# Second attention's output, router and dispatch in one stage, with expert rows gathered by a token list

## The chip, the core and the metric

One NeuronCore of a Trainium2 chip runs the whole network in one launch. Its engines work side by side and hand over by semaphores: PE (TensorE: matmuls and transposes; PEld is its weight load), DVE (VectorE), ACT (ScalarE), POOL (GpSimd) and SP (SyncE, which here only issues DMAs). The metric is the device time of one execution in microseconds (us), the median of several runs. The profile is one execution that the hardware profiler took.

## The reference

A tower of two blocks on 4 images of 512 tokens with 256 features, to which a class token per image is added after the first attention. Cut to the part that matters here:

```python
h = tok_attention(x)                                  # 16 heads of 16
h = concat([cls_tok, h], axis=1)                      # 4 x 513 tokens
h = h + rot_attention(layernorm(h))                   # causal, rotary; the "second attention"
# mixture of experts: 8 experts, 2 per token, hidden 512
x = layernorm(h).reshape(2052, 256)
topk_logits, topk_idx = top_k(x @ moe_router, 2)
weights = softmax(topk_logits)
out = zeros_like(x)
for each token t and its choice k, e = topk_idx[t, k]:
    gate, up = split(x[t] @ w13[e], 2)
    out[t] += weights[t, k] * ((silu(gate) * up) @ w2[e])
h = h + out
h = h + top_attention(layernorm(h))                   # causal, the 32 largest scores of a row only
h = h + second_experts(layernorm(h))                  # 8 experts, gated by a wide layer
```

## The kernel before

Tokens stand in 17 tiles: 16 of 128 tokens (`NT`) and one that holds the four class tokens. The program is a row of stages. A stage is a function that gives each engine its instruction list; engines run in their written order and wait on semaphores, and a barrier of all engines ends each stage. The stages in order: `begin`; `project` and `attend` for the first attention ("tok"); `attend_out` for it; `project` and `attend` for the second ("rot"); `attend_out` again; `route_moe`; `dispatch`; `run_gated_experts`; `gather_project`; `attend_top`; `last_experts`.

`attend_out` loads the output weights `wo` and bias `bo` at its start (L1812, L1813), and both PE and DVE wait for the two loads (`w_in`). Then for each tile n PE transposes the context (`turn`, L1823), ACT copies it (L1863), PE multiplies with `wo` (`project_tile`, L1832), DVE adds bias (L1897) and, for the second attention, the residual `h` (L1900), and normalises: bn_stats (L1909), bn_aggr (L1911), the root on ACT (L1869), reciprocal (L1915), and a tensor_scalar into `xn` (L1918), which is the tensor `ctx`. PE turns the normed tile (L1842) and ACT copies it to `xt` (L1876). For the second attention SP also issues the three loads of the expert weights here (`c.fetch`, 12 MB, tile `moe_w`).

`route_moe` loads the router, multiplies all 17 tiles with it (L2689: two channels of two weight loads each for a tile, so 68), and DVE finds the two largest logits of each token (`max` L2701, `max_index` L2704). `dispatch` turns the choices into places: DVE makes one-hot rows `chosen`, PE counts with a triangular and an all-ones matrix, DVE adds the counts up tile by tile (L1989, 17 steps that each wait for the one before), finds where each expert's tiles begin (L1998), and writes a row number for each of the 2 x 17 columns of tokens. Then POOL issues 34 indirect DMAs (L2036), each of which scatters 128 rows of 1 KB into the table `moe_xs` in DRAM, and waits for all of them.

`run_gated_experts` works through up to 40 tiles of 128 sorted rows, of which 38 hold tokens in this profile. SP loads rows i into one of two buffers (L2081) once PE has turned rows i-2 (`x_mm`), and stores the results y. PE turns the rows (L2120), multiplies with the owner expert's first matrix (L2131), and later with the second.

Rows that no token fills must be finite, so `attend` of the first attention clears two DRAM tables of 5 MB in the middle of its work (`clear`, tiles `moe_xs` and `last_xs`), on SP's DMA queue, ahead of the loads of later heads' queries and keys.

```python
if clear and s == G:
    for xs in c.xs.values():
        sp.dma_start(xs..., c.zeros[:, :, :].broadcast_to([P, TILES, D])).then_inc(c.xs_clear, 16)
```

Of the kernel before, what the change touches and what calls it, by code (L numbers as in the profile page):

```python
# [20 lines left out]
F32 = mybir.dt.float32  # L21
# [219 lines left out]
def project(c, tag, w, qkb, vb, cls, heads, rope=None, first=False):  # L241
# [9 lines left out]
    with c.stage() as st:  # L251
# [1517 lines left out]
def attend_out(c, tag, wo_dram, bo_dram, residual, cls, keep=None, fetch=()):  # L1769
# [6 lines left out]
    tiles = NT + (1 if cls else 0)  # L1776
    with c.stage() as st:
        wo = c.sbuf(st, f"{tag}_wo", [P, DC, D], F32)
        bo = c.sbuf(st, f"{tag}_bo", [P, D], F32)
        ctx_t = c.sbuf(st, f"{tag}_ctx_t", [P, 2, DC, P], F32)  # L1780
        summed = c.sbuf(st, f"{tag}_summed", [P, 2, D], F32)
# [5 lines left out]
        xn = keep if keep is not None else c.sbuf(st, f"{tag}_xn", [P, n_all, D], F32)  # L1787
# [3 lines left out]
        w_in = c.sem(st, f"{tag}_wo_in")  # L1791
# [4 lines left out]
        h_ok = c.sem(st, f"{tag}_h_ok")  # L1796
# [12 lines left out]

        @block.sync  # L1810
        def _(sp):
            sp.dma_start(wo[:, :, :], wo_dram).then_inc(w_in, 16)  # L1812
            sp.dma_start(bo[:, :], bo_dram.partition_broadcast(P)).then_inc(w_in, 16)  # L1813
            c.fetch(sp, fetch)

        @block.tensor
        def _(pe):
# [29 lines left out]
            pe.wait_ge(w_in, 32)  # L1847
# [42 lines left out]
        def _(dve):  # L1890
            def sums(n):
                r = rows(n)
                dve.wait_ge(o_mm, n + 1)
                if residual:
                    if n >= 2:
                        dve.wait_ge(h_ok, n - 1)
                    dve.tensor_tensor(summed[0:r, n % 2, :], ps_o[0:r, n % 2, 0:D], bo[0:r, :], ALU.add  # L1897
                                      ).then_inc(sum_ok, 1)
                    dve.wait_ge(sum_ok, n + 1)
                    dve.tensor_tensor(c.h[0:r, n, :], c.h[0:r, n, :], summed[0:r, n % 2, :], ALU.add  # L1900
                                      ).then_inc(h_ok, 1)
# [20 lines left out]
            dve.wait_ge(w_in, 32)  # L1922
# [9 lines left out]
def dispatch(c, tag, xn, idx):  # L1932
# [7 lines left out]
    n_all = NT + 1  # L1940
    with c.stage() as st:
        chosen = c.sbuf(st, f"{tag}_chosen", [P, 2, n_all, E], F32)
        both = c.sbuf(st, f"{tag}_both", [P, n_all, E], BF16)
        base = c.sbuf(st, f"{tag}_base", [P, n_all + 1, E], F32)
        begin = c.sbuf(st, f"{tag}_begin", [P, E + 1], F32)
        tiles = c.sbuf(st, f"{tag}_tiles", [P, E], F32)
        over = c.sbuf(st, f"{tag}_over", [P, E, n_all], F32)
        slot = c.sbuf(st, f"{tag}_slot", [P, n_all, E], F32)
        slot_in = c.sbuf(st, f"{tag}_slot_in", [P, n_all, E], F32)
        mine = c.sbuf(st, f"{tag}_mine", [P, 2, n_all, E], F32)  # L1950
        at = c.sbuf(st, f"{tag}_at", [P, 2, n_all], F32)
        has = c.sbuf(st, f"{tag}_has", [P, 2, n_all], F32)
# [3 lines left out]
        ps_total = c.psum(st, f"{tag}_ps_total", [P, S])  # L1956
        both_ok = c.sem(st, f"{tag}_both_ok")
        rank_mm = c.sem(st, f"{tag}_rank_mm")
        chain = c.sem(st, f"{tag}_d_chain")
        row_ok = c.sem(st, f"{tag}_row_ok")  # L1960
        sent = c.sem(st, f"{tag}_sent")
        block = st.enter_context(nc.Block())
        rank = ps_rank[:, 0:n_all * E].rearrange("p (n e) -> p n e", e=E)
        total = ps_total[:, 0:n_all * E].rearrange("p (n e) -> p n e", e=E)

        @block.vector
        def _(dve):
# [8 lines left out]
            for k in range(2):  # L1976
                then(dve.tensor_tensor(chosen[:, k, :, :],
                                       c.iota_e[:, :].rearrange("p (a e) -> p a e", a=1).broadcast_to([P, n_all, E]),
                                       idx[:, :, k:k + 1].broadcast_to([P, n_all, E]), ALU.is_equal))

                then(dve.tensor_tensor(chosen[:, k, :, :], chosen[:, k, :, :],
                                       c.valid[:, :].rearrange("p (n a) -> p n a", a=1).broadcast_to([P, n_all, E]),
                                       ALU.mult))
            dve.tensor_tensor(both[:, :, :], chosen[:, 0, :, :], chosen[:, 1, :, :], ALU.add).then_inc(both_ok, 1)
# [1201 lines left out]
```

## Time and profile before

| what | us |
|---|---|
| median of 3 runs | 1999.71 (1995.37 to 2009.43) |
| the profiled execution | 2001.38 |
| its span, first to last instruction | 1999.5 |
| second attention's `attend_out` starts | 678.22 |
| first expert tile's transpose on PE | 807.76 |

A row of the timeline gives the start, the duration, the engine, the line, the operation with its output and inputs, and in brackets how long the engine had been idle and what released it. Such times are from the span's start; the profiled execution's own time is 1.88 us longer than its span.

### The profile page before, as it was taken

How to read it: one execution, taken by the hardware profiler on the slowest of the kernel's cores; microseconds unless marked ns; L12 is line 12 of the kernel's file. 1: busy time of each engine (PE TensorE's matmuls, PEld its weight loads, DVE VectorE, ACT ScalarE, POOL GpSimd, SP SyncE). 2: the span in 40 equal slices, each digit the busy share in tenths (PEclk: the TensorE clock that was granted, in tenths of full speed). 3: DMA queues.
4: the chain of work that ended last, by engine and by line, in shares of the span. 5: the costliest groups of instructions: out<-in, count | busy, mean ns of one | idle time of the engine just before them, and what ended most of it. 6: DMA issues, size and time to landing. Idle time of an engine off the chain costs nothing. (4 is left out here: it accounts for less than half of the span.)

```text
span 1999.5 us, 35040 instructions
## 1 busy us (share of the span) xinstructions
PE 1456.5 (73%) x10387; PEld 860.4 (43%) x10420; DVE 1437.2 (72%) x4691; ACT 841.5 (42%) x2077; POOL 586.1 (29%) x1063
## 2 busy tenths in 40 slices
PE   7788887978888650799983477667776777766665
PEld 4222224534444440465642244454454454544554
DVE  4778885667777550111228799999999999999992
ACT  3366664215555420222222354455444544554532
POOL 3300000230000006000006244556555545555550
PEclk9799999978999875899996567777777666767768
DMA  5371220241221422111126310210021001300000
GB/s 165 104 254 52 58 68 9 73 117 47 49 59 36 162 99 84 38 42 47 42 66 189 81 28 9 77 28 10 20 64 49 10 20 27 107 1 12 1 1 13
DMA packets 81759, 120.86 MB, mean 60 GB/s; under 512 B 9112, under 2 KB 67392, under 8 KB 80836
## 3 DMA queue, kind: packets, MB, share of 16 engines
q1 hardware_dynamic: 78340, 110.60, 18.9%
q0 software_dynamic: 3264, 8.41, 1.3%
q8 instruction: 70, 1.15, 0.2%
q14 instruction: 85, 0.70, 0.1%
HBM read 74.11 MB, written 45.38 MB: 60 GB/s over the span
## 5 line engine op out<-in xcount | busy, mean ns | idle before, releaser
L1671 DVE MATCH_REPLACE8 top_left<-top_next,top_left 128x65 f32<-128x65 f32 (+15 forms) x768 | 322.0, 427 | 0.0
L1666 DVE MAX8 top_next<-top_left 128x8 f32<-128x65 f32 (+15 forms) x768 | 300.6, 431 | 0.1
L1126 POOL TENSOR_TENSOR top_e<-top_e,top_left 128x33 f32<-128x33 f32 (+3 forms) x254 | 188.9, 766 | 200.2 <-DVE top_left L1671 200.0
L1401 ACT ACTIVATE top_e<-top_ps_s,top_neg_max 128x129 f32<-128x129 f32 (+15 forms) x256 | 125.8, 492 | 191.0 <-POOL top_neg_max L1570 179.0
L735 DVE TENSOR_REDUCE tok_rowmax<-tok_ps_s 128x1 f32<-128x512 f32 x256 | 167.3, 688 | 34.5 <-PE tok_ps_s L577 31.9
L2231 DVE TENSOR_TENSOR moe_hid<-moe_act_gate,moe_ps_h 128x512 f32<-128x512 f32 x39 | 26.8, 688 | 220.1 <-ACT moe_act_gate L2192 220.1
L1244 PE MATMUL top_ps_pt<-ident,top_e 128*128 128x128 f32 x640 | 139.8, 348 | 27.6 <-POOL top_e L1126 12.8
L735 DVE TENSOR_REDUCE rot_rowmax<-rot_ps_s 128x1 f32<-128x128 f32 (+3 forms) x256 | 115.7, 488 | 48.6 <-PE rot_ps_s L580 45.6
L708 ACT ACTIVATE tok_et<-tok_ps_st 128x1024 f32<-128x1024 f32 x128 | 124.5, 1021 | 54.7 <-PE tok_ps_st L611 54.5
L2131 PE MATMUL moe_ps_h<-moe_w,moe_rows_t 128*128 x312 | 142.1, 598 | 0.4 <-issue 0.4
L1413 ACT ACTIVATE top_prob_t<-top_ps_pt 128x128 f32<-128x128 f32 (+3 forms) x256 | 104.8, 432 | 69.9 <-PE top_ps_pt L1244 69.3
L708 ACT ACTIVATE rot_et<-rot_ps_st 128x1024 f32<-128x1024 f32 (+3 forms) x128 | 88.0, 703 | 93.7 <-PE rot_ps_st L614 93.7
L1244 PEld LDWEIGHTS top_ps_pt<-ident,top_e 128*128 128x128 f32 x640 | 101.9, 181 | 55.1 <-issue 45.9
L1227 PE MATMUL top_ps_s<-top_ks,top_qs 96*32 96x1 bf16 (+7 forms) x1024 | 78.7, 325 | 55.0 <-DMA top_ks<-k_parts 42.8
L1653 DVE MAX8 top_raw<-top_ps_s 128x8 f32<-128x129 f32 (+15 forms) x256 | 100.8, 432 | 22.4 <-PE top_ps_s L1229 22.3
L577 PE MATMUL tok_ps_s<-tok_ks,tok_qs 96*128 96x512 bf16 x256 | 102.6, 412 | 18.9 <-DVE tok_rowmax L735 9.6
L1339 PE MATMUL top_ps_x<-gate_x_t,gate_wi 128*128 128x128 f32 (+1 forms) x512 | 99.8, 372 | 21.4 <-ACT top_next_va L1467 6.9
L1661 DVE MATCH_REPLACE8 top_left<-top_e 128x129 f32<-128x129 f32 (+15 forms) x256 | 107.5, 427 | 0.0
L1339 PEld LDWEIGHTS top_ps_x<-gate_x_t,gate_wi 128*128 128x128 f32 x512 | 93.5, 282 | 29.2 <-issue 25.3
L1258 PE MATMUL top_ps_pv<-top_prob_t,top_vs 128*32 128x128 f32 x1280 | 68.5, 361 | 50.3 <-ACT top_prob_t L1413 49.7
L1570 POOL TENSOR_SCALAR top_neg_max<-top_raw 128x1 f32<-128x1 f32 x256 | 53.5, 214 | 149.5 <-DVE top_raw L1653 145.9
L577 PE MATMUL rot_ps_s<-rot_ks,rot_qs 96*128 96x128 bf16 (+3 forms) x256 | 79.2, 332 | 24.7 <-DVE rot_rowmax L735 23.5
(355 smaller groups left out, 3141.3 us busy)
## 6 DMA issues: line engine op xcount, KB each, us to landing
moe_w<-in_moe_w SPq DMA_DIRECT2D x3, 4096.0 KB, 23.9
moe_xs<-zeros SPq DMA_DIRECT2D x1, 5120.0 KB, 20.7
last_xs<-zeros SPq DMA_DIRECT2D x1, 5120.0 KB, 33.8
moe_rows<-moe_xs SPq DMA_DIRECT2D x40, 128.0 KB, 2.2
moe_ys<-moe_y SPq DMA_DIRECT2D x38, 128.0 KB, 1.7
top_vs<-v_by_position SPq DMA_DIRECT2D x16, 256.0 KB
k_parts<-rot_parts SPq DMA_DIRECT2D x16, 192.4 KB, 3.3
rot_ks<-k_parts SPq DMA_DIRECT2D x16, 192.4 KB
```

Of the source, the lines that this page charges most:

```text
L577: mm = pe.matmul(ps_s[:, u % 2, 0:keys(qt)], lhs, k[0:PARTS * HD, h, k0:k0 + keys(qt)], start=True, stop=not causal)
L708: act.activation(et[:, kt % 2, 2 * pr:2 * pr + 2, q_from(kt):], ps_st[:, 2 * pr:2 * pr + 2, q_from(kt):], ACT.Exp).then_inc(exp_ok, 1)
L735: dve.tensor_reduce(rowmax[:, g % 2, u:u + 1], ps_s[:, u % 2, 0:keys(qt)], AX_X, ALU.max).then_inc(max_ok, 1)
L1126: eng.tensor_tensor(e[:, U % KEPT, 0:w], e[:, U % KEPT, 0:w], left[:, U % 4, 0:w], ALU.subtract).then_inc(prob_ok, 1)
L1244: mm = pe.transpose(ps_t[:, U % 2, ch * P:ch * P + P], e[:, U % KEPT, ch * P:ch * P + P], c.ident[:, :])
L1339: mm = pe.matmul(out[:, i * P:i * P + r], gate_wi[:, ch, f * P:f * P + P], x_t[:, ch, 0:r], start=ch == 0, stop=ch == DC - 1)
L1401: act.activation(e[:, U % KEPT, 0:keys(U)], row(U), ACT.Exp, bias=neg_max[:, U % 4:U % 4 + 1]).then_inc(e_ok, 1)
L1413: act.activation(prob_t[:, m % 2, 0:J + 1, :, QS * (U % 4):QS * (U % 4) + QS], ps_t[:, U % 2, 0:P * (J + 1)].rearrange("p (c h q) -> p c h ...
L1661: dve.match_replace(left[:, U % 4, 0:w], e8[:, U % 4, :], e[:, U % KEPT, 0:w], 0.0).then_inc(pick, 1)
L1666: dve.max(next8[:, U % 2, step // 2, :], left[:, U % 4, 0:keys(U)]).then_inc(pick, 1)
L1671: ins = dve.match_replace(left[:, U % 4, 0:w], next8[:, U % 2, step // 2 - 1, :], left[:, U % 4, 0:w], 0.0)
L2131: mm = pe.matmul(ps_h[:, k % 2, half, :], rows_t[:, k % 2, ch, :], w1[:, ch, bass.ds(e, 1), half * S:half * S + S].rearrange("p a n -> p ( ...
```

## The change

1. `attend_out`, `route_moe` and `dispatch` of the second attention become one stage, `attend_dispatch`. In one loop over tiles PE turns and projects tile n, turns the normed tile n-2, and routes tile n-3; DVE adds, normalises, and searches the two largest of tile n-4. Tiles are counted in groups (4, 4, 4, 3, 2): when a group has been searched, DVE makes its one-hot rows, POOL adds them up over tiles, PE ranks them, and DVE works out the place within an expert's tile, two iterations later.
2. There is no scatter and no table `moe_xs`. The normed rows go to DRAM in token order (`rot_normed`, 17 plain stores on SP). PE multiplies one-hot places with one-hot tiles, weighted with the token's number, which gives a list `ids`: for each expert tile and row, the token. `run_gated_experts` has POOL gather 128 rows by that list for each tile, into the same two buffers; SP keeps the stores.
3. Only `last_xs` is cleared.
4. Output weights, biases and the router are fetched with the other weights during the first attention. The second attention's bias is added to `h` by POOL during its `project` stage, so that DVE adds the projection straight to `h`.

```diff
 # project, POOL's list
+            if bias is not None:
+                pool.wait_ge(c.fetched, fetched)
...
                     pool.tensor_tensor(lo[:, k, span(k)], rest[:, k % 2, span(k)], mid[:, k, span(k)],
                                        ALU.subtract).then_inc(lo_ok, 1)
+                    if bias is not None:
+                        h = c.h[:, bass.ds(b * NQ + k, 1), :].rearrange("p a n -> p (a n)")
+                        pool.tensor_tensor(h, h, bias[:, :], ALU.add)
 # attend_out
-            sp.dma_start(wo[:, :, :], wo_dram).then_inc(w_in, 16)
-            sp.dma_start(bo[:, :], bo_dram.partition_broadcast(P)).then_inc(w_in, 16)
-            c.fetch(sp, fetch)
...
-            pe.wait_ge(w_in, 32)
+            pe.wait_ge(c.fetched, 16 * arrived)
 # attend_dispatch (new)
+    groups = [(0, 4), (4, 8), (8, 12), (12, 15), (15, n_all)]
+    chunks = [(0, 8), (8, 15), (15, n_all)]
...
+            c.fetch(sp, fetch)
+            for n in range(n_all):
+                r = rows(n)
+                sp.wait_ge(xn_ok, n + 1)
+                sp.dma_start(c.xn[n * P:n * P + r, :], c.ctx[0:r, n, :]).then_inc(x_sent, 16)
+            sp.wait_ge(x_sent, 16 * n_all)
...
+            def route(n):
+                pe.wait_ge(x_out, n + 1)
+                if n:
+                    pe.wait_ge(at_ok, n)
+                for ch in range(DC):
+                    mm = pe.matmul(ps_l[0:rows(n), 0:E], x_t[:, n % 2, ch, 0:rows(n)], router[:, ch, :],
+                                   start=ch == 0, stop=ch == DC - 1)
+                mm.then_inc(l_mm, 1)
+            def count(g):
+                a, b = groups[g]
+                if g < len(groups) - 1:
+                    pe.wait_ge(ahead_ok, b)
...
+                if g:
+                    pe.wait_ge(place_ok, g)
+                pe.matmul(ps_rank[:, 0:(b - a) * E], c.before[:, :], both[:, a:b, :], start=True, stop=False)
+                pe.matmul(ps_rank[:, 0:(b - a) * E], c.ones_bf[:, :], ahead[:, a:b, :], start=False, stop=True
+                          ).then_inc(rank_mm, 1)
...
+                            mm = pe.matmul(ps_ids[:, 0:2 * TILES], at_place[0:r, k, n, :],
+                                           by_row[0:r, k, n, :, :].rearrange("p a t -> p (a t)"),
+                                           start=n == 0 and k == 0, stop=n == n_all - 1 and k == 1)
...
+            for n in range(n_all + 4):
+                if n + 1 < n_all:
+                    turn(n + 1)
+                if n < n_all:
+                    project_tile(n)
+                if 2 <= n < n_all + 2:
+                    turn_normed(n - 2)
+                if 3 <= n < n_all + 3:
+                    route(n - 3)
+                if n - 5 in group_end and group_end[n - 5] < len(groups) - 1:
+                    count(group_end[n - 5])
+            count(len(groups) - 1)
+            row_numbers()
...
+            for n in range(n_all + 6):
+                if 4 <= n < n_all + 4:
+                    search(n - 4)
+                if n < n_all:
+                    sums(n)
+                    moments(n)
+                if 1 <= n <= n_all:
+                    normalise(n - 1)
+                if n - 4 in group_end:
+                    choose(group_end[n - 4])
+                if n - 6 in group_end and group_end[n - 6] < len(groups) - 1:
+                    places(group_end[n - 6])
+                    spread_places(group_end[n - 6])
 # dispatch, POOL's list
-                        pool.indirect_dma_start(
-                            out=c.xs[tag][:, :], out_offset=bass.IndirectOffsetOnAxis(ap=c.row[:, k, n:n + 1], axis=0),
-                            in_=xn[:, n, :], in_offset=None, bounds_check=TILES * P - 1, oob_is_err=False
-                        ).then_inc(sent, 16)
-                pool.wait_ge(sent, 16 * 2 * n_all)
 # run_gated_experts
-                sp.dma_start(rows[:, i % 2, :], c.xs[tag][i * P:(i + 1) * P, :]).then_inc(rows_in[i % 2], 16)
+            def gather_rows(i):
+                pool.indirect_dma_start(
+                    out=rows[:, i % 2, :], out_offset=None, in_=c.xn[:, :],
+                    in_offset=bass.IndirectOffsetOnAxis(ap=c.ids[:, i:i + 1], axis=0),
+                    bounds_check=NT * P + B - 1, oob_is_err=False).then_inc(rows_in[i % 2], 16)
+            gather_rows(0)
+            gather_rows(1)
+            used = used_tiles(pool)
+            for i in range(2, TILES):
+                if i < SURE_TILES + 2:
+                    pool.wait_ge(x_mm, i - 1)
+                    gather_rows(i)
 # program
-        c.xs = {t: nc.dram_tensor(f"{t}_xs", [TILES * P, D], F32, kind="Internal").ap() for t in ("moe", "last")}
+        c.xs = {t: nc.dram_tensor(f"{t}_xs", [TILES * P, D], F32, kind="Internal").ap() for t in ("last",)}
+        c.xn = nc.dram_tensor("rot_normed", [NT * P + B, D], F32, kind="Internal").ap()
+                get_rot = get_wo_tok + get_rot + get_wo_rot + [(router[:, :, :], a["router"])]
```

DVE's list in the middle of the second attention's output, before (one tile: add the bias, add to `h`, moments, and the normalising of the tile before):

```order
L1897 TENSOR_TENSOR rot_summed<-rot_ps_o,rot_bo 128x256
L1900 TENSOR_TENSOR h<-h,rot_summed 128x256
L1909 BN_STATS rot_stats<-h 128x6
L1911 BN_AGGR rot_mv<-rot_stats 128x2
L1915 RECIPROCAL rot_rstd<-rot_std 128x1
L1918 TENSOR_SCALAR ctx<-h,rot_mv,rot_rstd 128x256
```

and after, at tile 9, whose iteration also closes the second iteration after the first group's search (`rot_ps_l` holds one tile's logits):

```order
L2198 MAX rot_top<-rot_ps_l 128x8
L2200 MAX_INDEX rot_top_at<-rot_top,rot_ps_l 128x8
L2177 TENSOR_TENSOR h<-h,rot_ps_o 128x256
L2181 BN_STATS rot_stats<-h 128x6
L2183 BN_AGGR rot_mv<-rot_stats 128x2
L2187 RECIPROCAL rot_rstd<-rot_std 128x1
L2190 TENSOR_SCALAR ctx<-h,rot_mv,rot_rstd 128x256
L2227 TENSOR_TENSOR rot_mine<-rot_chosen,rot_ps_rank 128x2x32
L2231 TENSOR_REDUCE rot_rank<-rot_mine 128x2x4
L2232 TENSOR_TENSOR rot_whole<-rot_rank,steps 128x2x64
L2237 TENSOR_REDUCE rot_turn_no<-rot_whole 128x2x4
L2238 SCALAR_TENSOR_TENSOR rot_place<-rot_turn_no,rot_rank 128x2x4
```

One add went, and the search of the tile four back and, once in a group, the places came between a tile's normalising and the next tile's add.

POOL's list from the dispatch on, before (34 scatters behind the row numbers, and nothing in the expert stage):

```order
L2032 TENSOR_LOAD used
L2032 ISA x2
L2033 COMPARE_AND_BRANCH
L2036 DMA moe_xs<-ctx,row 5120x256 x34
L2033 UNCONDITIONAL_BRANCH
```

and after, from the last group that POOL adds up:

```order
L2156 TENSOR_TENSOR rot_both<-rot_chosen 128x24
L2162 TENSOR_TENSOR rot_ahead<-rot_ahead,rot_both 128x8 x3
L89 UNCONDITIONAL_BRANCH
L92 ISA
L2378 UNCONDITIONAL_BRANCH
L2381 DMA moe_rows<-rot_normed,ids 128x256 x2
L2355 TENSOR_LOAD used
L2355 ISA x2
L2381 DMA moe_rows<-rot_normed,ids 128x256 x32
```

The scatters are gone from between the stages; the expert stage's row loads came from SP to POOL, two ahead of the loop and the rest behind `x_mm`.

## Rows read from the trace of the kernel before

**Rows 1.** Timeline at the seams, from the second attention's output to the first expert tile.

```profile
678.22 0.36 SPq L1812 DMA_DIRECT2D rot_wo<-in_rot_wo  x1
...
683.51 0.69 PE L1823 MATMUL rot_ps_t<-ident,ctx 128*128 128x128 f32 x2 [4.59 <-DMA rot_bo<-in_rot_bo]
...
722.92 14.01 PE L2689 MATMUL moe_ps_l<-moe_router,xt 128*128 128x8 f32 x68 [2.63 <-DMA moe_router<-in_router]
...
742.73 0.30 DVE L1977 TENSOR_TENSOR moe_chosen<-iota_e,idx 128x136 f32<-128x136 f32 x1 [0.76 <-PEq L93]
...
805.65 4.38 SPq L2081 DMA_DIRECT2D moe_rows<-moe_xs  x4
807.76 0.29 PEld L2120 LDWEIGHTS moe_ps_x<-ident,moe_rows 128*128 128x128 f32 x2 [63.21 <-DMA moe_rows<-moe_xs]
```

**Rows 2.** Tiles moe_xs and moe_rows: ns min/median/max, first and last start in us.

```profile
L2036 POOL DMA_INDIRECT moe_xs<-ctx,row x34: 974/976/1270, 756.2 to 798.8; - x34
...
L2120 PE MATMUL moe_ps_x<-ident,moe_rows x80: 272/273/475, 807.8 to 1037.9; 128*128 128x128 f32 x80
```

**Rows 3.** Windows: PE, PEld, DVE, ACT, POOL busy, PE clock, DMA share, GB/s.

```profile
690.00:700.00 10.00, 7.57 (x41) 5.31 (x41) 9.10 (x31) 4.03 (x15) 0.00 (x0) 1.00 0.98 420
...
710.00:720.00 10.00, 6.70 (x34) 3.75 (x32) 9.24 (x31) 3.49 (x14) 0.00 (x0) 1.00 0.14 57
...
730.00:740.00 10.00, 6.92 (x36) 6.79 (x36) 3.01 (x41) 0.00 (x0) 0.00 (x0) 0.50 0.00 1
```

**Rows 4.** Timeline of SP, then of POOL, in the first attention.

```profile
98.19 14.80 SPq L547 DMA_DIRECT2D last_xs<-zeros  x1
...
137.14 0.62 POOL L562 COPY tok_vs<-tok_va 128x512 f32<-128x512 f32 x1 [13.66 <-PE tok_ps_pv L625]
155.73 0.62 POOL L562 COPY tok_vs<-tok_va 128x512 f32<-128x512 f32 x1 [17.97 <-PE tok_ps_pv L625]
```

**Rows 5.** Timeline: start of the first attention's output; end of the second's projection.

```profile
317.54 0.69 PE L1823 MATMUL tok_ps_t<-ident,ctx 128*128 128x128 f32 x2 [2.94 <-DMA tok_bo<-in_tok_bo]
...
426.26 2.18 POOL L451 TENSOR_TENSOR rot_parts<-rot_rest,rot_parts 128x513 bf16<-128x513 f32 x2 [3.16 <-ACT rot_parts L424]
```

**Rows 6.** Timeline of the second attention's output: first projection, and one later tile.

```profile
683.99 1.91 PE L1832 MATMUL rot_ps_o<-rot_wo,rot_ctx_t 128*128 128x256 f32 x4
...
711.50 0.42 DVE L1897 TENSOR_TENSOR rot_summed<-rot_ps_o,rot_bo 128x256 f32<-128x256 f32 x1
...
711.64 0.44 PE L1842 MATMUL rot_ps_x<-ident,ctx 128*128 128x128 f32 x2 [0.44 <-DVE ctx L1918]
...
711.95 0.43 DVE L1900 TENSOR_TENSOR h<-h,rot_summed 128x256 f32<-128x256 f32 x1
...
712.13 1.03 PE L1832 MATMUL rot_ps_o<-rot_wo,rot_ctx_t 128*128 128x256 f32 x4
...
713.47 0.42 DVE L1897 TENSOR_TENSOR rot_summed<-rot_ps_o,rot_bo 128x256 f32<-128x256 f32 x1
```

**Rows 7.** Timeline of DVE: a wide copy, the largest of 17 tiles, the chained sums.

```profile
435.02 1.23 DVE L824 COPY rot_v_cls<-rot_ps_st 128x1024 f32<-128x1024 f32 x1 [3.43 <-PE rot_ps_st L674]
...
737.35 1.25 DVE L2701 MAX8 moe_top<-moe_logits 128x8 f32<-128x8 f32 x17
...
744.94 3.30 DVE L1989 TENSOR_TENSOR moe_base<-moe_base,moe_ps_total 128x8 f32<-128x8 f32 x17 [0.56 <-PE moe_ps_total L2025]
```

**Rows 8.** Groups of POOL by form: busy us, mean ns of one, idle before.

```profile
L1141 POOL TENSOR_TENSOR h<-h,top_summed 128x256 f32<-128x256 f32 x15 | 11.2, 749 | 1.2
...
L1126 POOL TENSOR_TENSOR top_e<-top_e,top_left 128x33 f32<-128x33 f32 x16 | 4.1, 259 | 9.8 <-DVE top_left L1671 9.8
```

**Rows 9.** Timeline of POOL: indirect gathers in the stage behind the experts.

```profile
1046.61 1.36 POOL L2820 DMA_INDIRECT moe_got<-moe_ys,row  x1 [0.93 <-POOL moe_got L2814]
...
1051.40 1.00 POOL L2820 DMA_INDIRECT moe_got<-moe_ys,row  x1 [0.30 <-issue]
```

**Rows 10.** Tile moe_got: the 34 gathers from issue to landing.

```profile
DMA to landing us min/median/max: 2.7/3.1/7.7
```

More of the change, by code:

```diff
@@ L238, in load_step, with project @@
     load_keys(sp, c, b, g, k, loaded)
-def project(c, tag, w, qkb, vb, cls, heads, rope=None, first=False):
+def project(c, tag, w, qkb, vb, cls, heads, rope=None, first=False, bias=None):
     nc = c.nc
@@ L1974, in then @@
                 dve.wait_ge(chain, done[0])
[L1976 to L1983, printed above, removed]
@@ L1995, in _ @@
-            then(dve.tensor_reduce(tiles[:, :], over[:, :, :], AX_X, ALU.add))
-            then(dve.memset(begin[:, 0:1], 0.0))
-            for e in range(E):
-                then(dve.tensor_tensor(begin[:, e + 1:e + 2], begin[:, e:e + 1], tiles[:, e:e + 1], ALU.add))
-            then(dve.scalar_tensor_tensor(
-                out=slot_in[:, :, :], in0=begin[:, 0:E].rearrange("p (a e) -> p a e", a=1).broadcast_to([P, n_all, E]),
-                scalar=float(P), in1=base[:, 0:n_all, :], op0=ALU.mult, op1=ALU.add))
@@ L2002, in _ @@
-            then(dve.tensor_tensor(slot[:, :, :], slot_in[:, :, :], rank, ALU.add))
-            for k in range(2):
-                then(dve.tensor_tensor(mine[:, k, :, :], chosen[:, k, :, :], slot[:, :, :], ALU.mult))
-            then(dve.tensor_reduce(at[:, :, :], mine[:, :, :, :], AX_X, ALU.add))
-            then(dve.tensor_reduce(has[:, :, :], chosen[:, :, :, :], AX_X, ALU.add))
-            then(dve.scalar_tensor_tensor(out=at[:, :, :], in0=has[:, :, :], scalar=-float(NOWHERE),
-                                          in1=at[:, :, :], op0=ALU.mult, op1=ALU.add))
@@ new lines, in _ @@
+            then(dve.tensor_reduce(begin[:, :], shares[:, :, :], AX_X, ALU.add))
+            places(len(groups) - 1)
+            spread_places(len(groups) - 1)
+            then(dve.tensor_tensor(
+                mine[:, :, :, :], chosen[:, :, :, :], begin[:, 0:E].rearrange("p (k n e) -> p k n e", k=1, n=1
+                                                                              ).broadcast_to([P, 2, n_all, E]), ALU.mult))
+            then(dve.tensor_reduce(first_tile[:, :, :], mine[:, :, :, :], AX_X, ALU.add))
@@ new lines, in _ @@
+            then(dve.tensor_copy(c.used[:, :], begin[:, E:E + 1]))
+            then(dve.scalar_tensor_tensor(out=row_f[:, :, :], in0=tile_no[:, :, :], scalar=float(P), in1=place[:, :, :],
+                                          op0=ALU.mult, op1=ALU.add))
+            then(dve.tensor_tensor(c.row[:, :, :], row_f[:, :, :], nowhere[:, :].rearrange(
+                "p (k n) -> p k n", k=1).broadcast_to([P, 2, n_all]), ALU.add))
+            dve.wait_ge(ratio_ok, 1)
+            then(dve.tensor_scalar(one_more[:, :], ratio[:, :], 1.0, None, ALU.add))
@@ L2043, in run_gated_experts @@
+            then(dve.reciprocal(weight[:, 0, :], one_more[:, :]))
+            then(dve.tensor_tensor(weight[:, 1, :], ratio[:, :], weight[:, 0, :], ALU.mult))
+            dve.wait_ge(ids_mm, 1)
+            then(dve.tensor_copy(row_low[:, :], ps_ids[:, 0:TILES]))
+            then(dve.scalar_tensor_tensor(out=c.ids[:, :], in0=ps_ids[:, TILES:2 * TILES], scalar=float(P),
+                                          in1=row_low[:, :], op0=ALU.mult, op1=ALU.add))
 def run_gated_experts(c, tag, w1, w2, hidden):
@@ L3087, in program @@
             fetch = [(w13[:, ch], a["moe_w13"][:, ch]) for ch in range(DC)] + [(w2[:, :, :, :], a["moe_w2"])]
[L3088 to L3090 removed]
+            attend_dispatch(c, "rot", *wo_rot, router, idx, weight, fetch)
             run_gated_experts(c, "moe", w13, w2, MOE_HIDDEN)
```

475 lines of the change are left out of this document (315 added, 160 removed).

## Prediction

> **What bounds the kernel now.** I read the chain of waits first, and it is no help here: its pieces lie in the last part of the span, in the attention with 32 scores per row, which the change doesn't touch. So the places touched are read one by one from the timeline, by what each waits for last. In the seams of the middle [rows 1] the second attention's output stage begins at 678.22, PE then stands 4.59 us for the bias, the router multiplies from 722.92, dispatch starts at 742.73, the next stage's loads leave at 805.65 and PE turns the first expert rows at 807.76. These 129.5 us (807.76 - 678.22) are a serial piece: no other stage runs beside it. The windows [rows 3] show who fills it: DVE has 9.1 of 10 us while tiles are normalised, PE 6.9 of 10 while it routes at the lower clock, and nobody but POOL works in the scatter, 34 issues from 756.2 to 798.8 [rows 2]. Behind it the expert tiles run at (1037.9 - 807.8) / 39 = 5.9 us each [rows 2], on PE.
>
> **The change, part by part.** The sum is made against the profiled execution, 2001.4; the median is 1.7 lower.
>
> *A, one cleared table less.* The second clear kept SP's queue for 14.80 us, and the loads of later heads stood behind it. POOL's copies, one per head group, come every 13.66 + 0.62 = 14.3 us, but once 17.97 + 0.62 = 18.6 [rows 4]. With half the bytes the queue should be free before the keys are wanted: -4.3. If another thing made that step long, 0. I take -4.3.
>
> *B, weights of the first output stage.* PE stood 2.94 us for the bias [rows 5]. It now arrives in the first attention, on a queue idle by then: -2.9.
>
> *C, the bias on POOL.* 16 adds of 128x256 at 0.75 [rows 8], each behind a subtraction of 1.1 (two in 2.18 [rows 5]), plus one for the class rows. All but the last lie beside PE's projections. At the end the last subtraction starts one add later, 0.75, and an add and the class add follow, 1.5, beside SP's last stores: between 0 and +1.5, I take +0.6. What is queued behind is the barrier.
>
> *D, the fused stage.* Its length from start to the first expert transpose is built up.
>
> Start: turn, copy and first projection at the lower clock. Before, PE's second turn took 0.69 and the projection 1.91 [rows 6]; with 0.7 for the first turn and its copy, the first add is 3.3 us after the start.
>
> A tile: DVE needs 713.47 - 711.50 = 1.97 [rows 6], less one add (711.95 - 711.50 = 0.45), plus the search. A chained small operation takes 3.30 / 17 = 0.19 [rows 7], so two cost some 0.35: 1.87. PE needs from 711.64 to 712.13 + 1.03, so 1.52 [rows 6], plus four router weight loads: 14.01 / 68 = 0.21 each at the lower clock [rows 1, 3], half of that at the upper, 0.41. That is 1.93 on PE. PE waits for DVE's search (one buffer of logits) and DVE for PE's projection, but turn and projection lie between, so the two overlap; with 0.2 for handing over I take 2.15. Seventeen: 36.6.
>
> Groups: eight DVE instructions with 8 to 1024 columns. A cost of 0.19 plus 1.05 ns per column fits both ends ([rows 7]: 1.23 for 1024). 8 x 0.19 + 1488 x 1.05 ns = 3.1; three of these inside the loop, 9.3.
>
> POOL's counting: one add of 32 columns at 0.26 [rows 8] and four smaller ones in chain, 1.3 us, for which PE's `count` waits, with the next turn and projection queued behind it. PE would have been busy some 0.5 of that: +0.9 for each of three groups, 2.7.
>
> End: four more iterations without a projection, 0.9 each, 3.6. Then 43 DVE instructions in one chain (last group, first tiles, one-hot tiles, list): 43 x 0.19 + 6370 columns x 1.05 ns = 14.9. The 34 matmuls that make the list take at most 0.21 each; 16 of them run while DVE builds the second chunk, and the rest beside what DVE still has to do. Only 0.6 sticks out. Barrier 0.8 (the idle time at 742.73 [rows 1]), POOL's start 0.6, and the first gather, 3.1 from issue to landing [rows 10], with ends 2.7 and 7.7. The Trainium skill (DMA: Bandwidth & Descriptors, Anatomy of one DMA) fits such a DMA by 2.0 us plus its bytes at 436 GB/s, 2.3 us for 128 KB as an estimate; by it the sum would be 0.8 lower, and the rows say no.
>
> Sum: 3.3 + 36.6 + 9.3 + 2.7 + 3.6 + 14.9 + 0.6 + 0.8 + 0.6 + 3.1 = 75.5, so D is 129.5 - 75.5 = -54.0.
>
> What hides what: the expert weights are loaded at the start as before, at 420 GB/s, and the rate is down to 57 by the window after 710 [rows 3], more than 30 us before the stage's new end at 678.2 - 4.3 - 2.9 + 0.6 + 75.5 = 747. The 17 stores of normed rows queue behind them on SP and have the whole tail to land. In the expert loop a gather is issued when rows i-2 are turned, and its rows are needed two tiles later, 11.8 us; it takes 1.0 to issue and 2.7 to 7.7 to land [rows 9, 10]: nothing. SP's loads before landed in that shadow too. Behind the experts nothing is changed.
>
> Total: -4.3 - 2.9 + 0.6 - 54.0 = -60.6; 2001.4 - 60.6 = 1940.8, on the medians 1939.
>
> Bounds: A and C, +5.2 at worst. The tile on DVE's 1.87 alone gives -4.8, and if the groups' work fits in the time DVE waits for PE, -4.8 more; POOL's counting hidden, -2.7. The list's matmuls all behind DVE, +3; a first gather of 7.7, +4.6.
>
> **The rivals.**
>
> *1. The engines take turns.* Five engines in fixed order with two buffers each, and one for the logits: if DVE's search waits for PE's route, and PE's next projection waits for DVE, a tile costs PE's route plus DVE's work plus a handover, some 0.41 + 1.87 + 0.8 = 3.1 instead of 2.15: 17 x 0.95 = +16, 1955. For it: in the stage before, PE waits 0.44 us for DVE's normalised tile in every tile [rows 6]. Against: the turn and the projection don't depend on the search. Chance 0.20.
>
> *2. PE stays at the lower clock.* Then projection, two transposes and router cost 0.88 + 0.6 + 0.41 more per tile [rows 6], 17 x 1.9 = +32: 1971. Against: PE had 1.00 with 7.57 of 10 us busy [rows 3], and gets more work per tile. For it: the same PE with 6.92 busy of narrow router matmuls stood at 0.50 [rows 3]. Chance 0.06.
>
> *3. Slower than before: the gathers bind the experts.* Two buffers and one POOL instruction per tile: with a gather of G us from release to landing, a tile can't be shorter than (G + 0.4) / 2. Up to G = 11.4 it is hidden. To eat 60.6 us over 38 tiles it takes 1.6 us more a tile, G = 14.6; at 16, the tile is 8.2 and the time 1939 + 38 x 2.3 = 2026. For it: POOL makes the descriptors now, where SP loaded plain blocks, and a gather beside DVE's copies took 1.36 instead of 1.00 [rows 9]. Against: 7.7 was the longest of 34. The Trainium skill warns of just this (SBUF - State Buffer, Who interferes with whom, and the "DVE blocks DMA" trap): a two-port copy of DVE locks GpSimd out while it writes descriptors, and a DMA of 0.62 us took 3.1. The trace agrees in kind, with 0.36 us rather than 2.5. By the page a gather's issue, made five times longer, would be 5.0 as an estimate; this and 7.7 is 12.7, and only gathers that meet both ends would show. Chance 0.03.
>
> *4. The change doesn't do what it says*: the saving of the scatter is given back in the list's making, tail 25 us longer than added up (each chained instruction 0.77 instead of 0.19): 1964. Against: the chain of 17 has no such gap [rows 7]. Chance 0.03.
>
> **How the numbers follow.** The forecast has 0.68, the rivals 0.20, 0.06, 0.03 and 0.03. The likeliest is 1939. Its own range by the bounds, not all at once, is 1929 to 1950; with the first rival the range is 1928 to 1960. What a measurement can tell here is about 1%, 20 us. All cases but the third end below 1980; with a little kept for a stall that no row shows, faster 0.95, same 0.03, slower 0.02.
>
> **What would show it.** In the profile after: from the start of the fused stage to the first expert transpose 75 us (rival 1: over 88); DVE's adds 2.1 to 2.3 us apart outside the groups; PE's clock 1.00 in the middle of the stage (rival 2: 0.50); POOL's 40 gathers spread over the expert stage with PE's tiles still 5.9 us apart (rival 3: over 7); no copy of POOL in the first attention 18 us behind the one before; PE's first turn of the first output stage without a wait for a DMA. The prediction is wrong if the stage is over 95 us long, if the expert tiles slow down, or if anything behind 1044 takes another time than before.

## The result and the profile after

The changed kernel takes 1929.3 us (median of 4 runs, 1927.7 to 1935.0) where the kernel before took 2001.3: the ratio is 0.965, 95% interval 0.962 to 0.968. That is 72 us less; forecast were 60.6 less and 1939, with a range of 1928 to 1960. The profiled execution of after took 1935.0, the longest of the four, with a span of 1933.3. It is compared stage by stage with the one profile of before.

The timeline of after at the seams (start, duration, engine, line, operation, idle time before):

```profile
307.36 1.08 PE L1820 MATMUL tok_ps_t<-ident,ctx 128*128 128x128 f32 x4 [1.63 <-PEq L93]
...
340.14 3.30 POOL L446 MEMSET rot_va<- 128x3840 f32 x1 [89.67 <-POOLq L93]
...
423.03 1.80 POOL L563 MEMSET rot_ks<- 32x2052 bf16 x1 [1.10 <-POOLq L93]
...
667.56 0.63 PE L2030 MATMUL rot_ps_t<-ident,ctx 128*128 128x128 f32 x4 [2.44 <-PEq L93]
...
670.34 0.42 DVE L2177 TENSOR_TENSOR h<-h,rot_ps_o 128x256 f32<-128x256 f32 x1 [2.23 <-PE rot_ps_o L2039]
...
719.43 0.15 DVE L2200 FIND_INDEX8 rot_top_at<-rot_top,rot_ps_l 4x8 uint32<-4x8 f32 x1
...
733.69 0.20 DVE L2318 SCALAR_TENSOR_TENSOR ids<-rot_ps_t,rot_row_low 128x40 uint32<-128x40 f32 x1
735.86 1.30 POOL L2381 DMA_INDIRECT moe_rows<-rot_normed,ids  x1 [17.17 <-issue]
...
739.15 0.69 PE L2405 MATMUL moe_ps_x<-ident,moe_rows 128*128 128x128 f32 x2 [7.27 <-DMA moe_rows<-rot_normed,ids]
...
977.48 0.35 SPq L98 DMA_DIRECT2D top_w<-in_top_w  x1
```

The fused stage begins at 667.56 and the first expert rows are turned at 739.15: 71.6 us, where [rows 1] give 129.5. Its last search ends at 719.58, the list is written at 733.89, and POOL's first gather starts 1.97 later. All stages, each from such seams, with the letters of the prediction's terms:

| stage | before | after | difference | forecast |
|---|---|---|---|---|
| up to the first attention | 66.7 | 65.7 | -1.0 | 0 |
| first attention (A) | 247.5 | 241.7 | -5.8 | -4.3 |
| first output stage (B) | 35.1 | 32.8 | -2.3 | -2.9 |
| second projection (C) | 82.0 | 82.9 | +0.9 | +0.6 |
| second attention | 247.0 | 244.5 | -2.5 | 0 |
| output, router, dispatch (D) | 129.5 | 71.6 | -57.9 | -54.0 |
| experts, to the next stage's first load | 236.6 | 238.3 | +1.7 | 0 |
| the rest | 955.2 | 955.8 | +0.7 | 0 |
| span | 1999.5 | 1933.3 | -66.2 | -60.6 |

In the expert stage the gathers land in the shadow, as the view of the tile `moe_rows` shows (durations in ns; of the 40, all but the first took 992 to 998):

```profile
L2405 PE MATMUL moe_ps_x<-ident,moe_rows x80: 272/273/476, 739.1 to 970.6; 128*128 128x128 f32 x80
L2381 POOL DMA_INDIRECT moe_rows<-rot_normed,ids x40: 992/992/1299, 735.9 to 960.0; - x40
...
DMA to landing us min/median/max: 2.7/2.8/3.6
```

The tiles are (970.6 - 739.1) / 39 = 5.94 us apart (before 5.9, [rows 2]). The +1.7 of the expert stage isn't the gathers' doing as far as the runs show: with plain loads again (`e1_scatter`, below) the stage takes 237.3, and in the other kernels with one gather a tile, issued in that stage, 236.8 to 238.3.

### The profile page after: what moved, and what is told of

It reads as the page before. It is cut to its first block and busy times, and to the rows that moved or that the text cites. A ratio compares the mean times of both kernels' runs of the same rounds, so it can differ in the third digit from the quotient of the medians.

```text
span 1933.3 us, 35202 instructions
## 1 busy us (share of the span) xinstructions
PE 1459.6 (75%) x10462; PEld 857.0 (44%) x10463; DVE 1442.6 (75%) x4694; ACT 842.7 (44%) x2080; POOL 607.8 (31%) x1108
## 5 line engine op out<-in xcount | busy, mean ns | idle before, releaser
L1234 PE MATMUL top_ps_s<-top_ks,top_qs 96*32 96x1 bf16 (+7 forms) x1024 | 77.8, 322 | 55.2 <-DMA top_ks<-k_parts 43.5
L1346 PE MATMUL top_ps_x<-gate_x_t,gate_wi 128*128 128x128 f32 (+1 forms) x512 | 95.1, 359 | 22.8 <-ACT top_next_va L1474 8.2
L2381 POOL DMA_INDIRECT moe_rows<-rot_normed,ids x40 | 40.0, 1001 | 202.3 <-PE moe_ps_x L2405 184.8
L1346 PEld LDWEIGHTS top_ps_x<-gate_x_t,gate_wi 128*128 128x128 f32 x512 | 88.9, 270 | 30.2 <-issue 26.2
```

Of the source, the lines that this page charges most:

```text
L1346: mm = pe.matmul(out[:, i * P:i * P + r], gate_wi[:, ch, f * P:f * P + P], x_t[:, ch, 0:r], start=ch == 0, stop=ch == DC - 1)
```

## The experiments

**The theory** after the result: fusion and list each give a part of D, the list the larger; in a clean tile, one without a group's work, PE (some 1.93, as added up) and DVE (1.87, measured where it has no gap) run beside each other; the clear and the late weights were real costs; gathers have room. **The rivals**: the gain is the fusion's alone; the engines take turns; the long step of the first attention was an accident of one execution; gathers are near to binding. The edits are shown shortened.

How far a stage repeats has to be known first. `e10_unchanged` is the changed kernel once more.

> The changed kernel as it is, beside the run before it on the same chip: 1930. Its second profile shows how far each stage's length repeats: the stage 71.5 within 1.5, the second attention anywhere from 240 to 246.

It took 1928.5 (1924.8 to 1936.6), ratio 0.963 (0.961 to 0.965), and its fused stage 68.8 instead of 71.6, further off than the 1.5 that were expected. In six profiles whose loop is that of the changed kernel, the loop (from the first turn to the start of the last search) took 48.5 to 51.6 us, mean 50.3; the tail (from there to the first expert rows) took 20.0 to 20.2 where that too is unchanged. The difference goes with PE's clock behind a group's chain. A granted clock of 1.00 is TensorE's upper level, 2.4 GHz, and 0.50 the lower one, 1.2. The windows of after, and then of the repeat, whose stage begins 2.0 us later (columns: stretch, busy time of PE, PEld, DVE, ACT and POOL, granted clock, DMA share, GB/s):

```profile
685.00:690.00 5.00, 4.27 (x29) 3.28 (x27) 3.95 (x20) 1.90 (x8) 1.04 (x5) 1.00 1.08 465
690.00:695.00 5.00, 2.49 (x10) 2.18 (x11) 4.28 (x17) 1.24 (x5) 0.00 (x0) 0.78 0.97 416
695.00:700.00 5.00, 5.00 (x21) 4.16 (x20) 2.60 (x12) 0.85 (x3) 1.04 (x5) 0.54 0.84 271
```

```profile
680.00:685.00 5.00, 4.99 (x32) 3.81 (x31) 4.40 (x21) 2.22 (x9) 0.00 (x0) 1.00 0.98 421
685.00:690.00 5.00, 4.25 (x29) 3.44 (x29) 3.98 (x21) 2.08 (x8) 1.04 (x5) 1.00 1.01 433
690.00:695.00 5.00, 2.49 (x19) 1.84 (x18) 4.59 (x16) 0.84 (x3) 0.00 (x0) 1.00 0.98 416
695.00:700.00 5.00, 4.25 (x30) 3.38 (x30) 4.57 (x22) 1.92 (x8) 1.04 (x5) 1.00 1.12 419
```

In the repeat's first window, where no group is worked on, PE is busy for 4.99 of 5 us. In both executions PE stands for 2.51 us in the window from 690, until the search that is queued behind the first group's chain is done. In after the clock then falls, and DVE's next two adds come 3.49 and 3.31 us apart; in the repeat it stays, and they come 1.99 and 2.22 apart. A stage length is trusted below only beyond this spread.

**The scatter put back** (`e1_scatter`): the fused stage without the list; what follows is as before.

```diff
-            row_numbers()                      # PE: one-hot products
-            spread_places(g), at_tile, by_row  # DVE and ACT: their factors
+            for n, k: pool.indirect_dma_start(out=c.xs["moe"], ... c.row[:, k, n:n + 1], in_=c.ctx[:, n, :])
```

> The changed kernel with the list of tokens undone: the fused stage scatters its normalised rows into a cleared table, 34 issues by POOL, and the expert tiles load plain blocks, as before; the second table is cleared again in the first attention. Theory (fusion and list each give a part, the list the larger one): the loop 52.1 less three spreads of 1.2, 48.5; the tail 14.3 less the spreads and the list's tiles, 8.6; then the scatter as before, 51.6 from its first issue to the first expert transpose (807.8 - 756.2). Stage 109 us instead of 71.6, the first attention 5.8 longer for the clear: 1929 + 37 + 6 = 1972. Rival (the gain is the fusion's, and a scatter behind it would be cheap too, POOL's issues taking 1.0 instead of 1.25 in a quiet stage): stage under 98, time under 1960.

Measured 1971.8, ratio 0.987 (0.984 to 0.990). The stage took 107.0, the first attention, with both clears, 246.1. From its timeline, first and last scatter, then the loads and PE:

```profile
720.06 1.27 POOL L2147 DMA_INDIRECT moe_xs<-ctx,row  x1 [11.32 <-issue]
721.63 0.98 POOL L2147 DMA_INDIRECT moe_xs<-ctx,row  x1 [0.30 <-issue]
...
762.51 0.97 POOL L2147 DMA_INDIRECT moe_xs<-ctx,row  x1 [0.31 <-issue]
769.36 4.33 SPq L2332 DMA_DIRECT2D moe_rows<-moe_xs  x4
771.42 0.29 PEld L2371 LDWEIGHTS moe_ps_x<-ident,moe_rows 128*128 128x128 f32 x2 [59.00 <-DMA moe_rows<-moe_xs]
```

The scatter's 51.4 us (771.42 - 720.06) are those of before. So fusing gives 129.5 - 107.0 = 22.5 us, and the list another 107.0 - 71.6 = 35.4 (38.2 against the repeat), plus the clear. The rival (under 98) falls.

**The clear and the late weights put back** (`e2_clear_and_weights`):

```diff
-        c.xs = {... for t in ("last",)}
+        c.xs = {... for t in ("moe", "last")}
-                get_rot = get_wo_tok + get_rot + ...
+                attend_out(c, "tok", *wo_tok, get_wo_tok)    # SP fetches them there
```

> The changed kernel with terms A and B undone, everything else left: two tables are cleared in the first attention, and the weights of the first output stage are fetched in that stage. Theory: POOL's copy that came 18.6 us behind the one before and the later one of 15.6 both return, the first attention takes 247.5 instead of 241.7 (+5.8); the first output stage takes 35.1 instead of 32.8 (+2.3); time 1937. Rival (the long step was an accident of that one execution): attention 241.7 within 0.5, only the +2.3 shows, 1932.

Measured 1940.6 in one run; first attention 248.3, first output stage 34.8. Its timeline, SP's queue and POOL's copies:

```profile
96.14 14.36 SPq L554 DMA_DIRECT2D last_xs<-zeros  x1
110.60 14.33 SPq L223 DMA_DIRECT2D tok_qs<-q_parts  x3
...
134.14 0.61 POOL L569 COPY tok_vs<-tok_va 128x512 f32<-128x512 f32 x1 [13.65 <-PE tok_ps_pv L632]
153.43 0.62 POOL L569 COPY tok_vs<-tok_va 128x512 f32<-128x512 f32 x1 [18.68 <-PE tok_ps_pv L632]
```

the late copy of `e1_scatter`, which has both clears too, but the weights early:

```profile
155.07 0.61 POOL L569 COPY tok_vs<-tok_va 128x512 f32<-128x512 f32 x1 [18.04 <-PE tok_ps_pv L632]
```

and that of after:

```profile
107.55 5.08 SPq L223 DMA_DIRECT2D tok_qs<-q_parts  x3
...
136.04 0.61 POOL L569 COPY tok_vs<-tok_va 128x512 f32<-128x512 f32 x1 [13.66 <-PE tok_ps_pv L632]
150.30 0.61 POOL L569 COPY tok_vs<-tok_va 128x512 f32<-128x512 f32 x1 [13.65 <-PE tok_ps_pv L632]
```

With both clears a step of 19.3 us is back, and one of 18.7 in `e1_scatter`: 5.0 and 4.4 over the usual 14.3. The loads behind the clears keep the queue for 14.33 instead of 5.08. The attention takes 248.3 and 246.1, which is 2.8 to 7.3 us longer than the 241.0 to 243.3 of the kernels with one clear. The long step was no accident, and since `e1_scatter` shows it with the weights early, it belongs to the clear. The second long step of before (15.6) returned in neither run. The first output stage is 2.2 longer than one at the same clock (32.6 in `e5_search_first`, both at 0.90).

**The bias on DVE** (`e3_bias_dve`): one more add per tile there, none on POOL.

```diff
-                dve.tensor_tensor(h, h, ps_o, ALU.add)
+                dve.tensor_tensor(summed, ps_o, bo, ALU.add)
+                dve.tensor_tensor(h, h, summed, ALU.add)
```

> The changed kernel with term C undone: no bias adds on POOL in the second projection; DVE adds the bias in the fused stage, one more add of 0.45 us a tile. Theory (PE's 1.93 and DVE's 1.85 a tile run beside each other, with little slack on DVE): a clean tile 2.30 instead of 1.97, the loop 6 us longer, the projection 0.9 shorter, time +5. Rival 1 of the prediction (engines in turns, everything adds up): +7.7 in the loop. Rival (PE alone sets the pace and DVE has room): loop unchanged.

Measured 1939.0 in one run; loop 57.3, projection 81.3. Clean tiles of this kernel in the timeline, and then of after:

```profile
671.65 0.40 DVE L2182 TENSOR_TENSOR rot_summed<-rot_ps_o,rot_bo 128x256 f32<-128x256 f32 x1
...
673.96 0.40 DVE L2182 TENSOR_TENSOR rot_summed<-rot_ps_o,rot_bo 128x256 f32<-128x256 f32 x1
```

```profile
679.59 0.40 DVE L2177 TENSOR_TENSOR h<-h,rot_ps_o 128x256 f32<-128x256 f32 x1
...
681.58 0.42 DVE L2177 TENSOR_TENSOR h<-h,rot_ps_o 128x256 f32<-128x256 f32 x1
```

2.31 against 1.99 apart (four tiles in a row: 2.32 against 1.96 in the mean). 0.44 us more DVE work lengthen a tile by 0.36: DVE had some 0.1 of slack beside PE, as the theory has it; PE alone doesn't set the pace. The loop is 5.7 longer than that of after, 7.0 than the mean of 50.3: the rival's 7.7 isn't excluded by that sum, but by the tile, which would be 3.1 us and one add more if the engines took turns.

**The group's chain out of the loop** (`e4_places_last`):

```diff
-                if n - 6 in group_end and ...: places(g); spread_places(g)   # in the loop
+            for g in range(len(groups) - 1): places(g); spread_places(g)     # behind it
```

> The changed kernel with the work on ranks and places of the first four groups moved out of the loop to its end (same instructions, later). Theory (a group's DVE chain of 3.1 us inside the loop costs more than itself, because PE stands 2.5 us behind the search, and its clock falls for the next two tiles): the loop loses 3 x 4.5 = 13, the tail gains 9, the stage is 4 us shorter, PE's clock 1.00 through the loop. Rival (DVE's work is what counts, wherever it stands): stage the same within 1 us. Second rival (the clock falls in the loop in any case): stage longer by up to 4.

Measured 1935.2 in one run; loop 40.6, tail 27.6, stage 68.1. The clock stays at 1.00 until 5 us before the loop's end. The chains of three groups cost some 10 us in the loop and 7.6 behind it: the sign of the theory, but 68.1 is within 0.7 of the shortest unchanged stage, so its 4 us aren't shown.

**The search ahead of the chain** (`e5_search_first`):

```diff
-                if 4 <= n < n_all + 4: search(n - 4)     # first in DVE's iteration
                 sums(n); moments(n); normalise(n - 1)
+                if 3 <= n < n_all + 3: search(n - 3)     # choose and places follow
```

> The changed kernel with one move in DVE's order: the search of a tile's logits stands at the end of an iteration ahead of the group's chain, not behind it at the start of the next. Same instructions. Theory (PE stands 2.5 us in each of two groups because the search is queued behind the group's chain, and then runs the next two tiles at the lower clock): PE's wait for the search, 7.9 us in 5 times, falls under 3; the clock stays at 1.00 in the middle; the loop is 5 to 8 us shorter, the time 1923. Rival (DVE's sum sets the pace, PE's wait is slack): loop shorter by less than 1.5, time 1929.

Measured 1931.6, ratio 0.966 (0.965 to 0.968); loop 48.7. The theory fell. PE's waits in the loop (us in total, times, longest), of after:

```profile
PE rot_ps_l L2058 <- DVE rot_top_at L2200: 7.9, 5, 2.5
...
PE rot_ps_x L2049 <- DVE ctx L2190: 0.9, 2, 0.6
```

and with the search first:

```profile
PE rot_ps_x L2049 <- DVE ctx L2190: 4.8, 4, 2.2
...
PE rot_ps_l L2058 <- DVE rot_top_at L2200: 1.9, 1, 1.9
```

The wait for the search is gone and stands one tile later, at the normalised tile, which DVE also makes only after its chain. What costs is then the chain on DVE, not the order around it; the better versions below test that.

**More gathers** (`e6_gather3`, `e6_gather5`): each tile's gather three or five times, the extra ones into spare buffers, and PE waits for all.

```diff
+                for to in [rows[:, i % 2, :]] + [spare[:, r, i % 2, :] for r in range(R - 1)]:
```

> The changed kernel with every gather of the expert loop made three times (twice more into a spare buffer, and PE waits for all three): POOL issues 120 instead of 40. Theory (a gather has 11.4 us from release to wanted; three take 3 x 1.29 to issue and 2.8 to land, 6.7): tiles stay 5.94 apart, the stage is longer only by the start, some 3 us; time 1932. Rival 3 of the prediction (the gathers are near to binding): tiles over 6.3, time over 1945.

Three: 1935.6 in one run, tiles 6.0 apart.

> The same with five gathers a tile. Theory: POOL itself becomes the bound, 5 x 1.29 = 6.45 us a tile instead of 5.94, 38 x 0.5 = +20 and some 5 at the start: 1955. Rival 3 (landing grows with the queue, or issues are made longer by DVE's copies): tiles over 7, time over 1975. Third case (issues overlap with something that the trace shows as a gap): tiles 5.94, 1935.

Five: 1969.0 in one run, tiles 6.76 apart. POOL's timeline in the middle:

```profile
853.75 1.00 POOL L2383 DMA_INDIRECT moe_rows<-rot_normed,ids  x1 [0.31 <-issue]
855.06 0.99 POOL L2383 DMA_INDIRECT moe_spare<-rot_normed,ids  x1 [0.30 <-issue]
...
860.26 1.00 POOL L2383 DMA_INDIRECT moe_rows<-rot_normed,ids  x1 [0.30 <-issue]
```

Back to back at 1.30, so POOL sets the pace: 200 issues from 732.5 to 997.1 are 6.6 us a tile. With the tile 0.31 over the 6.45 expected, 39 tiles make 12 of the 14 us by which the time was over; the rival's 7 a tile and 1975 weren't reached. Three fit, five don't, and one leaves POOL idle for 4.9 of 5.9 us. An issue never grew over 1.01 us behind the first, although POOL issued all through DVE's copies of the results, one a tile. The rule of the Trainium skill in rival 3 (SBUF — State Buffer, Who interferes with whom) has a DVE instruction in a two-port mode lock GpSimd out; no issue of these 200 shows that, and whether those copies ran in such a mode no run here shows, so the rule isn't tested here.

**Versions with a shorter stage.** Since the chain on DVE costs, part of it went to POOL, which is idle there (`e7_pool_spread`: the one-hot rows of the first four groups).

```diff
-                dve.tensor_tensor(at_place[:, :, a:b, :], iota_p..., place..., ALU.is_equal)
+                for n, k: pool.tensor_scalar(at_place[:, k, n, :], iota_p, place[:, k, n:n + 1], None, ALU.is_equal)
```

> The changed kernel with the one-hot rows of a group's places (1024 columns on DVE, 1.2 us) made by POOL, in eight instructions of 128 columns, for the first four groups. Theory (a group's DVE chain in the loop is what costs, 3.1 us of which this is 1.2): loop 3.5 us shorter, tail 1 shorter. Rival (POOL's eight instructions come late to the list or get in DVE's way): stage the same or longer.

Measured 1923.1 in one run; loop 45.0, tail 20.0, stage 65.0. The loop is 5.3 shorter than the mean, the stage 3.8 shorter than the shortest unchanged one. The tail didn't gain.

`e8_prefetch` has POOL issue the first two gathers at the end of the fused stage, ahead of the barrier. For that DVE writes the list ahead of its last seven small operations.

```diff
+            pool.wait_ge(ids_ok, 1); pool.wait_ge(x_sent, 16 * n_all)
+            gather_rows(0); gather_rows(1)     # in attend_dispatch, not in run_gated_experts
```

> The changed kernel with the first two gathers issued by POOL at the end of the fused stage, as soon as the list is there, ahead of the barrier and beside DVE's last small operations. Theory (the first gather's 3.3 us and the barrier's 2.0 lie one behind the other, and can lie side by side): first expert transpose 2 to 3 us earlier. Rival (the barrier now waits for POOL's two issues of 1.3 and 1.0): within 0.5 us of the same.

Measured 1925.5 in one run, stage 71.4, tail 21.4: the tail lost 1.2 to 1.4. Its timeline:

```profile
723.97 0.20 DVE L2320 SCALAR_TENSOR_TENSOR ids<-rot_ps_t,rot_row_low 128x40 uint32<-128x40 f32 x1
...
726.68 0.99 POOL L1919 DMA_INDIRECT moe_rows<-rot_normed,ids  x1 [0.30 <-issue]
...
732.25 0.66 PE L2408 MATMUL moe_ps_x<-ident,moe_rows 128*128 128x128 f32 x2 [8.63 <-issue]
```

PE starts 4.6 us behind the end of POOL's last issue and waits for no DMA by then. The barrier takes that long; what in it does stays open.

`e9_all_three` joins the two with the search first.

> Search first, POOL's one-hot rows and the early gathers together. Theory: the three add, 2.5 + 4.5 + 2 = 9 us off the stage, some 62 us, and 1921 in all. Rival (they save the same wait twice): stage 66, 1926.

Measured 1930.0, ratio 0.964 (0.961 to 0.966); loop 43.6, tail 23.4, stage 67.0 where the theory had 62 and the rival 66. The loop gained; the tail lost 3.4, 1.4 of it as in `e8_prefetch` and 2.0 to POOL's rows, for which the list's second part waited:

```profile
713.60 10.99 POOL L2032 TENSOR_SCALAR rot_at_place<-rot_iota_p,rot_place 128x128 bf16<-128x128 f32 x14
...
724.74 1.47 PE L2111 MATMUL rot_ps_t<-rot_by_row,rot_at_place 128*128 128x80 bf16 x18 [1.77 <-POOL rot_at_place L2032]
```

Of these 14 instructions nine took 0.60 us. The five others took 0.92 to 1.50, all while DVE worked on rows of 272 to 640 columns. One of each kind, and DVE's instruction beside the second:

```profile
717.07 0.60 POOL L2032 TENSOR_SCALAR rot_at_place<-rot_iota_p,rot_place 128x128 bf16<-128x128 f32 x1
...
719.91 0.82 DVE L2314 TENSOR_TENSOR rot_at_tile<-iota_t,rot_tile_no 128x640 bf16<-128x640 f32 x1
720.04 1.16 POOL L2032 TENSOR_SCALAR rot_at_place<-rot_iota_p,rot_place 128x128 bf16<-128x128 f32 x1
```

At 0.60 each, the 14 would have ended some 2.9 us sooner. What made POOL's rows late, then, are the instructions that ran beside DVE's wide ones; why those take longer no run here tests.

`e11_pool_three` has the search first and POOL's rows for three groups; it leaves the fourth group on DVE and the gathers in their stage. Against `e9_all_three`, without the gathers:

```diff
-            spread(pool, len(groups) - 2)
+            spread(dve, len(groups) - 2)
```

> Search first, and POOL's one-hot rows for the first three groups only (the fourth stays on DVE, since POOL took 0.68 us for each instruction of 128 columns and came 1.8 us late to the list's second part); no early gathers. Theory: the loop as in the run with all three, 43.6, the tail as unchanged, 20.0; stage 64, time 1922. Rival (what the loop gains is inside what a stage varies by from run to run): stage 67 or more, time 1927 to 1930.

Measured 1924.5 (1921.4 to 1928.6), ratio 0.962 (0.959 to 0.965); loop 43.5, tail 21.1, stage 64.6. The stage is shorter than the unchanged ones (68.8 to 71.6 in three profiles) by 4 to 7 us, beyond their spread. That the whole kernel is faster isn't shown: the interval overlaps that of the unchanged kernel (0.961 to 0.965).

## Why the prediction was right, and where its sizes were off

**D** held in its mechanism. Its terms against after: start to last search 55.5 forecast (3.3 + 36.6 + 9.3 + 2.7 + 3.6), 52.0 measured; DVE's tail chain with the list 15.5, 14.3 measured (733.89 - 719.58); barrier and POOL's start 1.4, 2.0; first gather 3.1, 3.3. The most mis-sized term is the tile: 2.15 was 1.96, and the "0.2 for handing over" isn't there, which makes 17 x 0.19 = 3.2 us. A group's work was smaller than added up too. DVE's adds around the first group's chain in after:

```profile
688.32 0.42 DVE L2177 TENSOR_TENSOR h<-h,rot_ps_o 128x256 f32<-128x256 f32 x1 [0.74 <-PE rot_ps_o L2039]
...
692.69 0.40 DVE L2177 TENSOR_TENSOR h<-h,rot_ps_o 128x256 f32<-128x256 f32 x1
```

That is 4.37 - 1.96 = 2.4 over a clean tile, and with the 0.2 for the one-hot rows two tiles earlier 2.6, where 3.1 stood; POOL's counting cost the 0.74 that DVE waits at 688.32, where 0.9 stood. Against that, two or three tiles behind a group at the lower clock took up to 3.1 us, which the sum didn't have. In the repeat, with fewer of them, D is 68.8.

**A**: -4.3 forecast, -5.8 in the two profiles; with the clear put back the late copy alone costs 4.4 and 5.0, the whole stage 2.8 to 7.3. The forecast counted one late copy; before had a second, 15.6 instead of 14.3, which is gone in after. **B**: -2.9 forecast, -2.3 in the two profiles and 2.2 by the weights put back. **C**: the profiles say +0.9, but with the adds the projection took 81.9 to 82.2 at a granted clock of 0.94, and without them 82.0 (before) and 81.3 (`e3_bias_dve`) at the same clock: a cost under 1 us, which these runs can't tell from none.

**The second attention**, 2.5 us shorter with the same code, goes with the clock. The windows of that stage in after and in `e11_pool_three`:

```profile
423.00:667.60 244.60, 200.52 (x1929) 106.58 (x1930) 174.42 (x468) 121.00 (x193) 16.89 (x21) 0.91 0.20 47
```

```profile
420.40:660.30 239.90, 190.53 (x1913) 103.43 (x1929) 174.43 (x467) 121.10 (x193) 16.90 (x21) 0.94 0.20 47
```

In 13 profiles of kernels with the same attention it took 239.9 to 245.6, the longer the lower the granted clock (0.94 to 0.90); the one profile of before has 247.0 at 0.89. Whether the change itself raises that clock can't be told from one profile of before. The rest behind the experts, untouched as well, took 955.1 to 965.1 in these profiles, so the +0.7 of after says nothing.

The time is 11 us lower than forecast. The two profiles show 5.6 of that (66.2 less instead of 60.6), chiefly D's 3.9 and the second attention's 2.5, beside smaller parts that nearly cancel; the profiled execution of after was 5.7 above its median. D's 3.9 to 6.7 and the second attention are where the whole 11 are to be looked for; for the executions without a profile that is argued, not shown. With 1929.3 in a range from 1928, it is partly luck that these misses stayed inside: no bound of the forecast has the second attention in it.

**The rivals.** 1 (engines in turns): no, 1.96 us a tile; only at a group's chain does PE stand 2.5 us for the search. 2 (lower clock): in part, behind groups, with some 3 us between executions instead of 32. 3 (gathers bind): no, it takes more than three gathers a tile. The 1.36 that the prediction held against DVE's copies was a stage's first issue, and a first issue took 1.30 in after as well, with DVE idle since 733.89; the two issues behind it took 1.26 beside those copies, so what the copies can have cost is nearer to 0.26 than to 0.36. 4 (the list's making): no, the chain took 14.3. What was to show it did, in the main: 71.6 us against 75, adds 1.87 to 2.08 apart against 2.1 to 2.3, clock 1.00 in the middle but not throughout, tiles 5.94 apart, and PE's first turn of the first output stage without a DMA wait. The late copy is gone; the 18.9 us ahead of the fifth copy, at the attention's start, stand in both kernels (18.94 and 18.89), and the prediction hadn't counted them.

## What to carry to other kernels

Where serial stages each keep one engine busy, add up per engine what a tile costs in the joined loop: the larger sum, without an allowance for handing over, was within 0.1 us of the tile. A scatter of 34 issues behind the routing cost 51 us because nobody could start before it ended; a list of row numbers lets the consumer gather tile by tile in its own shadow, at 1.3 us of POOL's time a tile of 5.9. When a wait comes from a long chain on a shared engine, moving the waiting step in front of it only moves the wait; take work off the engine, as POOL's rows did, and not beside wide operations of DVE, where POOL's took up to 1.50 us instead of 0.60.

## What was not expected of the hardware

- PE stood for 2.51 us for the same search, at the same place of the loop, in two executions of one kernel; behind it the granted clock was 0.54 over 5 us in one, and stayed at 1.00 in the other.
- POOL's comparison of 128 columns took 0.60 us, where DVE did 1024 in 1.23; beside DVE's operations on 272 to 640 columns, five of 14 took 0.92 to 1.50.
- A stage that ends with POOL's gathers let PE start 4.6 us after the end of the last issue; with DVE's last instruction at the end, POOL itself started 2.0 us after it.
